# Softmax maxima of two heads turned together, scores run two heads ahead, in a fused cross-attention and expert-network kernel

## The reference, cut to what matters

```python
b, s1, _ = x.shape                                  # 4, 512
q = _ln((x @ Wq + bq).reshape(b, s1, H, HD), ...)   # 16 heads of 32
k = _ln(kv[..., :HD]); v = kv[..., HD:]             # 496 rows of context
ctx = _attn(qT, k, v) + _attn(qT, k_dca, v_dca)     # a second softmax over the last 16 rows
x = x + (ctx @ Wo + bo)
scores = softmax(layernorm(x) @ gate_w.T)           # 64 experts, the best 6 of each row
buf[e, slot] = rows of expert e                     # up to 384 rows of an expert
eo = (silu(buf @ w_gate) * (buf @ w_up)) @ w_down   # per expert
y = scatter_add(eo * weight) + shared_swiglu(x)
x = x + y
```

## Time and profile before

| what | value |
|---|---|
| median of three runs | 1764.61 us |
| the profiled execution: device time | 1762.85 us |
| its span, first to last instruction | 1761.1 us |
| PE busy | 1693.0 us, 96% of the span |
| PE weight loads | 1539.8 us, 87% |
| DVE, ACT, POOL busy | 62%, 58%, 43% |
| mean granted TensorE clock | 0.982 |
| chain that ended last | 1% of the span, in the scatter-adds of the thirds |

### The profile page before, as it was taken

The page is one execution under the profiler, slowest core; times in us unless marked ns, Lnnn a source line. Parts: engine busy times, 40 slices in busy tenths (PEclk is TensorE's granted clock), DMA queues, the critical chain, the costliest instruction groups (busy, mean ns, idle before and its releaser), DMA issues. The chain is left out here.

```text
span 1761.1 us, 35834 instructions
## 1 busy us (share of the span) xinstructions
PE 1693.0 (96%) x11782; PEld 1539.8 (87%) x11782; DVE 1090.3 (62%) x2157; ACT 1028.3 (58%) x1871; POOL 757.9 (43%) x719
## 2 busy tenths in 40 slices
PE   4899999999999999999999999999999999999995
PEld 3588888888888888989999999999999999999984
DVE  7555656777566665443666666666666666666664
ACT  4567766666545553222566666666666666666664
POOL 7513222334223230242245555555555555455554
PEclk8899999999899999999999999999999999999997
DMA  5543433433222532312577777777777777777766
GB/s 189 160 117 91 119 105 97 121 95 98 83 84 79 177 107 87 122 38 86 181 227 232 209 214 226 218 210 223 223 216 205 228 221 213 222 232 206 215 198 212
DMA packets 149083, 289.87 MB, mean 165 GB/s; under 512 B 29199, under 2 KB 66319, under 8 KB 139649
## 3 DMA queue, kind: packets, MB, share of 16 engines
q1 hardware_dynamic: 116112, 238.21, 41.9%
q0 software_dynamic: 32880, 50.51, 13.7%
HBM read 243.73 MB, written 64.52 MB: 175 GB/s over the span
## 5 line engine op out<-in xcount | busy, mean ns | idle before, releaser
L2188 POOL DMA_INDIRECT out<-y,ids_s x128 | 209.9, 1640 | 280.3 <-ACT y L2323 254.8
L2448 PE MATMUL ps<-xt_hi,gu_hi 128*128 128x256 f32 (+1 forms) x1856 | 303.5, 285 | 0.6 <-issue 0.6
L2448 PE MATMUL ps<-xt_lo,gu_hi 128*128 128x256 f32 (+1 forms) x1856 | 289.8, 278 | 0.0
L2448 PE MATMUL ps<-xt_hi,gu_lo 128*128 128x256 f32 (+1 forms) x1856 | 289.2, 278 | 0.0
L2223 DVE TENSOR_TENSOR gu_lo<-raw_gu,gu_hi 128x1408 fp32r<-128x1408 f32 (+2 forms) x132 | 214.6, 1625 | 112.5 <-ACT gu_hi L2220 109.3
L1121 ACT ACTIVATE prob<-ps 128x512 f32<-128x512 f32 x256 | 152.2, 597 | 191.4 <-PE ps L1428 169.6
L2448 PEld LDWEIGHTS ps<-xt_hi,gu_hi 128*128 128x128 f32 (+1 forms) x1856 | 250.6, 181 | 9.0 <-issue 3.0
L2448 PEld LDWEIGHTS ps<-xt_lo,gu_hi 128*128 128x128 f32 (+1 forms) x1856 | 244.4, 181 | 0.0
L2448 PEld LDWEIGHTS ps<-xt_hi,gu_lo 128*128 128x128 f32 (+1 forms) x1856 | 244.2, 181 | 0.0
L2168 POOL DMA_INDIRECT xg<-h_rows,ids_g x128 | 191.6, 1497 | 115.2 <-POOL ids_g L2163 50.6
L2280 ACT ACTIVATE h_hi<-h 128x256 fp32r<-128x256 f32 (+1 forms) x240 | 100.6, 419 | 224.0 <-DVE h L2349 223.4
(11 more groups left out here) (316 smaller groups left out, 3000.3 us busy)
## 6 DMA issues: line engine op xcount, KB each, us to landing
raw_gu<-in_w_gu SPq DMA_DIRECT2D x71, 1408.0 KB, 6.7
raw_d<-in_w_d SPq DMA_DIRECT2D x71, 512.0 KB
raw_d<-in_w_d SPq DMA_DIRECT2D x71, 192.0 KB
qs<-qk_rows SPq DMA_DIRECT2D x192, 64.0 KB, 2.2
ks<-qk_rows SPq DMA_DIRECT2D x192, 64.0 KB, 2.0
xa<-in_x SPq DMA_DIRECT2D x16, 256.0 KB, 3.0
qk_rows<-k_hi SPq DMA_DIRECT2D x16, 256.0 KB, 2.2
qk_rows<-k_lo SPq DMA_DIRECT2D x16, 256.0 KB, 2.5
```

The source lines that it names most:

```text
L2188: pool.indirect_dma_start(out=out, out_offset=bass.IndirectOffsetOnAxis(B.ids_s[:, p, k:k + 1], 0), in_=B.y[:, p, k, :], in_offset=None, b ...
L2448: last = pe.matmul(gu_banks(it, c)[half], gu_columns(w, it, half, d, c), x[:, x_p, d, 0:W], start=i == 0, stop=i == len(steps) - 1)
```

## The change

- PE makes the scores two heads ahead: `opened(n)` and `half1(n)` now do those of n+2. The front does those of head 1 as well, and heads 62 and 63 do none. DVE's `maxima` follow, each one head later in its number at the same place.
- The maxima of heads n and n+1 are turned together for even n: four transposes of 64 columns instead of twice four of 32. `nmax` is laid out with the two heads side by side. ACT copies both heads' rows one after the other, `shift_rows(n)` and `shift_rows(n + 1)`, ahead of the first exponential of head n.
- `shift_turned` waits for the logits at n % 4 == 2 and for the positions of one unit before at n % 4 == 0; `route_logits` and `route_pos` wait until the rows of the pair are copied.
- DVE's low part of Q, `rest(u + 4, ...)`, goes ahead of the second maxima of its head.
- From unit 10 on (no tile u+6), `k_turned(u + 5)` goes behind `third_key`.
- In the thirds, GpSimd gathers block 3 ahead of the scatter of the last expert, the copies of weights and row numbers get a function `columns` and are made for block b+1 between the wait for the scatter-add before and block b's own scatter-add, and the gather (of b+4) comes behind the scatter-add. One block more is gathered at the end than before.

```diff
-        nmax = sb("nmax", [P, 2, T, 32], F32R)
+        nmax = sb("nmax", [P, T, 2, 32], F32R)
...
                     maxima(0, 0)
                     maxima(0, 1)
+                    maxima(1, 0)
+                    maxima(1, 1)
...
-                maxima(n + 1, 0)
+                maxima(n + 2, 0)
                 residual(u - 5)
-                maxima(n + 1, 1)
+                rest(u + 4, q_full, q_hi, q_lo, q_high, q_low, q_out)
+                maxima(n + 2, 1)
                 take_logits(u - 6)
-                rest(u + 4, q_full, q_hi, q_lo, q_high, q_low, q_out)
...
-                act.activation(qs[96:128, n % RING, :], ps[0:32, TRB, :], ACT.Copy).then_inc(nmT_in.sem, 1)
+                o = n % 2 * 32
+                act.activation(qs[96:128, n % RING, :], ps[o:o + 32, TRB, :], ACT.Copy).then_inc(nmT_in.sem, 1)
...
                 shift_rows(n)
+                shift_rows(n + 1)
                 exps(n, 0)
...
                 shift_rows(n + 2)
+                shift_rows(n + 3)
                 deviations(u)
                 exps(n + 2, 0)
...
-                pe.wait_ge(nmax_ready.sem, nmax_ready.value(n, 2))
+                pe.wait_ge(nmax_ready.sem, nmax_ready.value(n + 1, 2))
...
-                if n % 4 == 1 and tile(u - 6):
+                if n % 4 == 0 and tile(u - 7):
+                    pe.wait_ge(pos_taken.sem, pos_taken.value(u - 7, 1))
+                if n % 4 == 2 and tile(u - 6):
                     pe.wait_ge(logit_taken.sem, logit_taken.value(u - 6, 1))
-                if n % 4 == 3 and tile(u - 6):
-                    pe.wait_ge(pos_taken.sem, pos_taken.value(u - 6, 1))
                 for t in range(T):
-                    last = pe.transpose(ps[0:32, TRB, t * P:(t + 1) * P], nmax[:, n % 2, t, :].bitcast(F32), ident[:])
-                last.then_inc(nmT_ready.sem, 1)
+                    pair = nmax[:, t].rearrange("p a c -> p (a c)").bitcast(F32)
+                    last = pe.transpose(ps[0:64, TRB, t * P:(t + 1) * P], pair, ident[:])
+                last.then_inc(nmT_ready.sem, 2)
...
             def opened(n):
-                shift_turned(n)
-                scores(n + 1, 0)
+                if n % 2 == 0:
+                    shift_turned(n)
+                scores(n + 2, 0)
...
-                scores(n + 1, 1)
+                scores(n + 2, 1)
...
                 scores(0, 0)
                 front_q_turned(4)
                 scores(0, 1)
+                scores(1, 0)
+                scores(1, 1)
...
-                k_turned(u + 5)
+                if tile(u + 6):
+                    k_turned(u + 5)
                 third_key(n + 2)
+                if not tile(u + 6):
+                    k_turned(u + 5)
...
             thirds["gather_first"](pool, 2)
+            thirds["gather_first"](pool, 3)
+            thirds["columns"](pool, FIRST)
             scatter(pool, it)
...
+    def columns(pool, b):
+        e = expert(pool, b)
+        pool.tensor_copy(B.wsl3[:, b.p:b.p + 1], B.w[:, bass.ds(e * CB + 2, 1)]).then_inc(w_copied.sem, 1)
+        pool.tensor_copy(B.ids3s[:, b.p:b.p + 1], B.ids[:, bass.ds(e * CB + 2, 1)]).then_inc(s_copied.sem, 1)
...
         def body(b):
-            e = expert(pool, b)
-            pool.tensor_copy(B.wsl3[:, b.p:b.p + 1], B.w[:, bass.ds(e * CB + 2, 1)]).then_inc(w_copied.sem, 1)
-            pool.tensor_copy(B.ids3s[:, b.p:b.p + 1], B.ids[:, bass.ds(e * CB + 2, 1)]).then_inc(s_copied.sem, 1)
-            pool.wait_ge(xt_ready.sem, xt_ready.value(b.j + 1, 1))
-            gather(pool, b + 3)
             if b.q:
                 pool.wait_ge(added.sem, added.value(b.j - 1, 16))
                 pool.sem_inc(y_free.sem, 1)
...
                 pool.sem_inc(y_free.sem, 1)
+            columns(pool, b + 1)
             pool.wait_ge(s_copied.sem, s_copied.value(b.j, 1))
             pool.wait_ge(y_taken.sem, y_taken.value(b.j, 1))
             pool.sem_inc(passed, 1)
...
                 compute_op=ALU.add).then_inc(added.sem, 16)
+            pool.wait_ge(xt_ready.sem, xt_ready.value(b.j + 2, 1))
+            gather(pool, b + 4)
         many = each(pool, body)
         for p in range(2):
-            pool.wait_ge(rows_in[p].sem, (many + (4 - p)) // 2 * 16)
+            pool.wait_ge(rows_in[p].sem, (many + (5 - p)) // 2 * 16)
```

More of the change, by code:

```diff
@@ L659, in maxima @@
                 t = slice(2 * half, 2 * half + 2)
-                dve.tensor_reduce(nmax[:, n % 2, t, 0], ps[:, SCB:SCB + 2, 0:MAIN], AX, ALU.max, negate=True)
-                dve.tensor_reduce(nmax[:, n % 2, t, 1], ps[:, SCB:SCB + 2, MAIN:S], AX, ALU.max, negate=True)
+                dve.tensor_reduce(nmax[:, t, n % 2, 0], ps[:, SCB:SCB + 2, 0:MAIN], AX, ALU.max, negate=True)
+                dve.tensor_reduce(nmax[:, t, n % 2, 1], ps[:, SCB:SCB + 2, MAIN:S], AX, ALU.max, negate=True)
                 dve.drain().then_inc(nmax_ready.sem, 1)
@@ L943, in heads_vector @@
                 xt_rest(u + 6)
-                maxima(n + 2, 0)
+                maxima(n + 3, 0)
                 route_max(u - 6)
@@ L949, in heads_vector @@
                 at_rest(u - 4)
-                maxima(n + 2, 1)
+                maxima(n + 3, 1)
                 route_top(u - 6)
@@ L953, in heads_vector @@
                 route_mask(u - 6)
-                maxima(n + 3, 0)
+                maxima(n + 4, 0)
                 scales(u)
-                maxima(n + 3, 1)
+                maxima(n + 4, 1)
                 take_pos(u - 6)
@@ L960, in heads_vector @@
                 route_code(u - 6)
-                maxima(n + 4, 0)
+                maxima(n + 5, 0)
                 rest(u + 5, k_full, k_hi, k_lo, k_high, k_low, k_out)
                 route_slots(u - 6)
-                maxima(n + 4, 1)
+                maxima(n + 5, 1)
                 route_weights(u - 6)
@@ L1314, in heads_scalar @@
                 ctx_high(u + 6)
-                shift_rows(n + 1)
                 exps(n + 1, 0)
@@ L1334, in heads_scalar @@
                 turned_full(u + 5, SB1, trk_ready, k_full, 2, True, k_low)
-                shift_rows(n + 3)
                 exps(n + 3, 0)
@@ L1500, in route_logits @@
                 pe.wait_ge(h2T_in.sem, h2T_in.value(j, 1))
+                pe.wait_ge(nmT_in.sem, nmT_in.value(4 * (j + 6) + 1, 1))
                 if j >= 1:
@@ L1537, in route_pos @@
                 pe.wait_ge(logit_taken.sem, logit_taken.value(j, 1))
+                pe.wait_ge(nmT_in.sem, nmT_in.value(4 * (j + 6) + 3, 1))
                 if j >= 1:
@@ L2645, in gather_first @@
         else:
-            pool.wait_ge(xt_ready.sem, xt_ready.value(0, 1))
+            pool.wait_ge(xt_ready.sem, xt_ready.value(k - 2, 1))
         gather(pool, FIRST + k)
@@ L2804, in tensor @@
         each(pe, body, many)
-    return dict(how_many=how_many, sync=sync, gather_first=gather_first, y_freed=y_freed, gpsimd=gpsimd, act_gu=act_gu, act_d=act_d,
+    return dict(how_many=how_many, sync=sync, gather_first=gather_first, columns=columns, y_freed=y_freed, gpsimd=gpsimd, act_gu=act_gu, act_d=act_d,
                 act_x=act_x, silu=silu, high=high, scalar=scalar, dve_gu=dve_gu, dve_x=dve_x, dve_d=dve_d, mix=mix,
```

## The result

The changed kernel takes 1793.48 us, the median of 6 runs (1783.22 to 1802.95), against 1764.26 for the kernel before on the same chips. The ratio is 1.017 (95% interval 1.014 to 1.020). I had predicted 1771.4 within 1757 to 1777, so slower was right and the size was not: the loss is 29 us where I had 7.

A forecast was written before the change was run, and what follows sets the result against it. PE was taken to bound the kernel, in attention loop and expert items. Terms of -9.9, +5.3, +6.2, +4.5, 0 and +1, less 0.3 for late heads, gave +6.8 on 1764.6: 1771.4 us, range 1757 to 1777.

The forecast's parts named there:

- Term 4: Behind PE's wait for head 63's rows, the clock falls to half for a stretch: +4.5 us.
- Term 1: Attention loop: turning two heads' maxima together spares PE 0.38 us a pair, over 26 pairs: -9.9 us.
- Term 2: End of the front: head 1's scores ahead of the loop wait for DVE's maxima and delay the turn: +5.3 us.
- Term 3: End of the heads: PE wants head 63's rows one head sooner, before they land, and waits: +6.2 us.
- Term 5: Head 42: a wait of about 1.0 us replaces one of 1.1, and the clock falls as before: 0 us.
- rival A: The clock doesn't fall in head 42: -6.7 us against the forecast, 1764.7 us; chance 0.20.
- Term 6: The thirds: an earlier gather saves, while `columns` between scatter-adds and one extra gather cost: +1 us (-5 to +5).
- Rival C: PE's margin at the clock is gone elsewhere: one more fall at 5.9 us, 1777.3, or thirds at their upper end; chance 0.10.
- the step against the change: Head 63's rows, wanted one head sooner with SP's order unchanged, come late and PE waits: +6.2 us.

The follow-up runs named there:

- single_turn: The changed kernel with each head's maxima turned alone again, 32 columns at a time, scores still two heads ahead; 1788.7 us, ratio 1.018.
- double_turn: The changed kernel with the four transposes of each pair issued twice in a row; 1806.9 us, ratio 1.024.
- tail_old: The changed kernel with the code of the thirds as in the kernel before; 1787.4 us, ratio 1.014.
- front_one: The changed kernel with the front's end as before, heads 0 and 1 turned singly, the two-head lead taken up in head 1; 1795.3 us, ratio 1.017.
- mended: The changed kernel with head 63's rows loaded ahead of the experts' weights, and the front's end and thirds as before; 1774.7 us, ratio 1.008.
- rows_later: The kernel before, with head 63's rows loaded only once the last turned scores of head 61 are done; 1783.1 us, ratio 1.011.
- copies_apart: The changed kernel with the odd head's copy of maxima on ScalarE moved behind the even head's first exponential; 1844.3 us, ratio 1.044.
- before_order_ring: The kernel before with Q's low part early, K's turn late in the last units and head 63's rows loaded early; 1759.2 us, again 1762.8 us.

## Why the prediction was wrong, step by step

The direction came out, and the size did not, for two steps that failed. Term 4 priced the clock behind the late rows at 4.5 us, and it costs 14 to 17.5 in the three kernels where PE is on time for them. And every other fall was put at nothing in the sum: the second copy on ScalarE was counted for heads 0 and 42 alone, where the runs show it delaying PE in head 46 as well, with the clock falling there in all six kernels that keep the two copies side by side; whether that wait is what makes it fall is open.

- **Term 1, right in mechanism, too big.** Predicted 0.38 a pair. The four transposes of 64 columns take 472.45 to 472.81, 0.36, where I had 0.38, and the odd head spares its 0.35. But over units 1 to 9 the gain is 4.7 us in 18 pairs, 0.26, the lower bound. Head by head the starts of the scores show where the rest went: heads 10 and 11 together fall from 16.78 to 16.32 us, while heads 8 and 9 stay at 14.12 and 14.14. There a new wait of 0.23 us behind the exponentials, which the second copy delays, takes half of it; where the other half goes is open.
- **Term 2, right.** Scores of head 0 to the turn take 9.70 us, 4.8 more than before; I had 5.33. What I did not ask is what the clock does there: it stayed at half for 23.9 us and not 10.2, and unit 0 lost another 4.3 us. Not the waits of term 2 bring this, for single_turn has them, with 13.65 us at half and nothing lost over unit 0. It goes with the turn in pairs: double_turn loses 4.4 us over unit 0 as well.
- **Term 3, right where PE is not late already** (6.3, 6.4 and 6.7 us in three kernels, 6.2 predicted), and nearly hidden in the changed kernel's profiled execution (0.69; 2.8 in tail_old's, where a fall at 582 had made PE late).
- **Term 4, the mechanism right and the size wrong**: 4.5 us predicted from 13.65 at half. The stretches last 41.0 us in single_turn and 47.8 in double_turn. From unit 15's first scores to the end of the heads these take 21.3 and 23.9 us more than the kernel before; less their waits of 6.3 and 6.4, the term is 15 and 17.5 (front_one's, by the same sum, 14.4). I took the length from a fall in the middle of the loop, where heads are full; in the last heads PE works between waits and the clock did not come back before their end.
- **Term 5, wrong; rival A was right.** The wait did turn from one of 0.85 into gaps of 0.64 and 0.22, as worked out, but the clock held: -6.4. That it held isn't settled by those gaps: in mended it fell at 446.9 behind gaps of 0.64, 0.23 and 0.40.
- **Term 6, in its range by this profile, but not by its sum.** +4.1, where I had +1 (-5 to +5); by all the traces some 6, outside it. `columns` costs what I took or a bit less: from a landing at 1741.93 to the next issue at 1744.15 are 2.2 us, and in the kernel before, from 1734.65 + 7.18 = 1741.83 to the issue at 1743.03, 1.2; at the others it is 1.9 to 2.1 against 1.0. Block 0's scatter-add is 0.9 us further behind the experts' last than before. The earlier gather gave back what I had said: from block 0's scatter-add to block 1's are 6.4 us and were 8.5. Two more steps grew by 0.6 and 1.5, with landings that differ between the traces. What I had too small is the end. The gather made once more is issued 2.7 us behind the last scatter-add. That scatter-add has landed by 1774.0, but GpSimd comes to its last waits only at 1777.3. From its issue to the end are 12.7 us and not 9.6, +3.1 where I had 0 to +1.5. This stretch is 12.69 us in all eight profiled kernels with the new thirds, and 9.4 to 11.9 in the twelve with the old:

```profile
1751.48 1.57 POOL L2670 DMA_INDIRECT out<-y,ids3s  x1 [1.07 <-issue]
...
1769.50 1.60 POOL L2685 DMA_INDIRECT out<-y,ids3s  x1 [0.66 <-issue]
1772.21 1.09 POOL L2648 DMA_INDIRECT xg<-h_rows,ids  x1 [0.91 <-POOL ids L2645]
```

  (The first row is the kernel before, with nothing behind it.)
- **Rival C is what came, and it failed by its price and chance.** It had "one more fall" at 5.9 us and 0.10. There came two (481 and 573) and a longer one in the front, and the last heads, together some 62 us more at half clock by the medians, or 26 us. The range rested on the clock as one event with one length, though the kernel before already had a fall behind a gap of only 0.85 in a loop that is 98% busy. That it came out slower is in part luck: at equal clock the change costs 0 to 2 us, the late rows, which I called the step against the change, cost 0.69 us of wait in the profiled execution, and two falls that stand in no term (481 and 573) come before them.

The Trainium skill ("TensorE: Matmul & The Clock Gate", Why this matters for your kernels) warns of long idle gaps between bursts of matmuls. The traces agree for the waits ahead of head 63, of 6.3 us in single_turn and 3.8 in rows_later. They show more than that: the fall at 573.43 stands behind a gap of 0.22 us, at 570.45, and PE had no longer gap than that in the 15 us before. Such a gap isn't enough by itself, for the kernel before has the same one, as the row shows, and keeps its clock there; so does mended, at 571.14. And double_turn's clock fell at 522.6 with no gap over 0.15 us in the 11 us before. What decides between these cases no run here shows.

```profile
569.01 0.41 PE L1444 MATMUL ps<-v_last,prob 128*128 128x66 f32 x2 [0.23 <-DVE pv L673]
```

## What to carry to other kernels

When PE is over 95% busy and the profile shows clock near 1, price each new gap on PE by what a forced gap costs in the same stretch, not by its length: here 3.8 us of wait cost 18, and 0.4 us at the same place, in one profiled execution, nothing. Moving two small operations together on a helper engine is not free, when that engine has its longest block (here roots with two table loads) right behind them; nor was it here to move them apart (copies_apart, 1844 us). And before calling a version faster, compare at equal clock: before_order_ring was ahead by 0.2% in one set of runs and level in the next.

## What was not expected of the hardware

- The same program fell into two clusters, 1752.6 to 1754.9 and 1770.7 to 1778.2 us (before_order_ring, measured again, 12 runs), with 35 to 46 and 74 to 103 us at half clock. The two clusters are some 20 us apart; only a run of the lower one was profiled, so which falls make the upper one isn't shown.
- The time at half clock explains the scatter of the kernel before to about 1.5 us (1.1 to 1.6 in five sets of runs, about lines of 0.31 to 0.43 us for each us).
- Repeating 128 transposes in place (double_turn) gave no clock back (130 us at half, 125 without). Four more cost 0.43 us: eight take 479.61 to 480.40, where four took 0.36.
